# Eight weighted key rows summed by one strided reduction instead of three adds

## The reference

```
kx     = modulated_linear(x, s, k_aff_w, k_aff_b, k_w, k_b).reshape(B, N, 16, 8)
scores = einsum('bnhd,bnjd->bnhj', kx, kx) / sqrt(8)
A      = softmax(scores, axis=-1)
out    = einsum('bnhj,bnjd->bnhd', A, kx).reshape(B, N, 128)
```

## Time and profile before

| | |
|---|---|
| time, median of 3 runs | 597.94 us (597.91 to 598.32) |
| profiled execution | 596.94 us, span 595.1 us |
| busy: TensorE matmul | 575.1 us (97%), 4516 instructions |
| busy: VectorE | 483.7 us (81%), 1026 |
| busy: ScalarE | 372.0 us (63%), 855 |
| busy: GpSimd | 288.1 us (48%), 248 |
| VectorE's three adds of eight rows, L349, L358, L360 | 52.4, 19.2 and 13.9 us, 32 of each |
| GpSimd's three adds, L1063 | 116.8 us, 96 |
| mean granted clock of TensorE | 0.989 |

### The profile page before, as it was taken

The page is one execution under the profiler, slowest core; times in us unless marked ns, Lnnn a source line. Parts: engine busy times, 40 slices in busy tenths (PEclk is TensorE's granted clock), DMA queues, the critical chain, the costliest instruction groups (busy, mean ns, idle before and its releaser), DMA issues. The chain is left out here.

```text
span 595.1 us, 15251 instructions
## 1 busy us (share of the span) xinstructions
PE 575.1 (97%) x4516; PEld 492.3 (83%) x4516; DVE 483.7 (81%) x1026; ACT 372.0 (63%) x855; POOL 288.1 (48%) x248
## 2 busy tenths in 40 slices
PE   8999999999999999999999999999998997799998
PEld 8888888888888888888888888888887896466775
DVE  4235888898989898988889898989898788777776
ACT  1767767777777677777777767777775321534443
POOL 1011666666666666666666666666666563000000
PEclk9999999999999999999999999999999977999999
DMA  7300000000000000000000000000000000000004
GB/s 240 86 2 2 1 3 2 0 0 0 0 0 0 0 0 0 0 0 0 0 0 0 0 0 0 0 0 0 0 0 2 1 1 0 1 1 0 0 0 141
DMA packets 9364, 7.18 MB, mean 12 GB/s; under 512 B 1089, under 2 KB 8833, under 8 KB 9217
## 3 DMA queue, kind: packets, MB, share of 16 engines
q1 hardware_dynamic: 9344, 6.94, 3.9%
HBM read 4.84 MB, written 2.10 MB: 12 GB/s over the span
## 5 line engine op out<-in xcount | busy, mean ns | idle before, releaser
L1068 POOL TENSOR_TENSOR pair<-kx 128x1152 f32<-128x1152 f32 x32 | 82.2, 2568 | 167.4 <-DVE shifted L388 158.4
L580 PE MATMUL bank_a<-v,prob 128*128 128x65 f32 x1024 | 128.5, 274 | 1.5 <-ACT prob L814 0.8
L580 PEld LDWEIGHTS bank_a<-v,prob 128*128 128x128 f32 x1024 | 121.8, 192 | 6.3 <-ACT prob L814 3.2
L1063 POOL TENSOR_TENSOR mix_hi<-mix_hi 128x512 f32<-128x512 f32 (+2 forms) x96 | 116.8, 1217 | 7.5
L271 DVE TENSOR_REDUCE row_max<-bank_s 128x4 bf16<-128x512 f32 x128 | 88.9, 694 | 26.2 <-PE bank_s L555 25.3
L814 ACT ACTIVATE prob<-bank_t 128x512 f32<-128x512 f32 x128 | 68.9, 589 | 6.9 <-PE bank_t L570 4.7
L587 PE MATMUL misc<-yT,wq_sb 128*128 128x128 f32 x512 | 69.6, 279 | 0.5 <-DVE yT L419 0.5
L570 PE MATMUL bank_t<-qT,kT 64*128 64x256 f32 x512 | 65.7, 376 | 0.0
L1056 POOL TENSOR_TENSOR mix_hi<-weight,kx 128x1024 f32<-128x1024 f32 x32 | 64.1, 2002 | 3.1 <-ACT weight L814 3.1
L282 DVE TENSOR_TENSOR att<-bank_a,recip_den 128x256 f32<-128x256 f32 x128 | 54.4, 425 | 13.0
L587 PEld LDWEIGHTS misc<-yT,wq_sb 128*128 128x128 f32 x512 | 62.0, 191 | 3.6 <-DVE yT L419 0.7
(11 more groups left out here) (149 smaller groups left out, 998.9 us busy)
## 6 DMA issues: line engine op xcount, KB each, us to landing
out<-acc_all SPq DMA_DIRECT2D x8, 256.0 KB, 2.3
x_all<-in_xT SPq DMA_DIRECT2D x1, 1024.0 KB, 9.7
w_sb<-in_w SPq DMA_DIRECT2D x2, 512.0 KB
x_all<-in_xT SPq DMA_DIRECT2D x1, 768.0 KB, 7.5
wq_sb<-in_wq SPq DMA_DIRECT2D x1, 512.0 KB, 6.1
wpost_sb<-in_wpost SPq DMA_DIRECT2D x1, 512.0 KB, 9.6
x_all<-in_xT SPq DMA_DIRECT2D x1, 256.0 KB, 3.3
b_rows<-in_b SPq DMA_DIRECT2D x16, 4.0 KB
```

Source lines behind the costliest of these rows:

```text
L580: last = mm(att_bank(g)[:, w, :], prob[:, g % 2, w, :], v1[:, j, g, :], start=(w == 0), stop=True, skip_group_check=True)
L1063: G.tensor_tensor(mix_hi[:, 0:r, :], mix_hi[:, 0:r, :], mix_hi[:, r:2 * r, :], ALU.add).then_inc(s_hi, 1)
L1068: G.tensor_tensor(pair[:, :, :], bass.AP(kx2, jc * 2 * P, [[4 * P, P], [0, SHIFTS], [1, P]]), bass.AP(kx2, jc * 2 * P, [[4 * P, P], [MD, S ...
```

## The change

VectorE's three adds over `mix_lo` become one `tensor_reduce`. It reads all eight rows, with the rows as the innermost axis (128 outputs of 8 elements, each 128 elements apart in memory), and writes the sum to a new tile `mix_part` of 128 x 128. It stands where the first of the three adds stood, ahead of L353. The other two adds, which stood behind the reciprocal, go. `mixed()` reads `mix_part` in place of the first row of `mix_lo`. The semaphore `s_lo` now counts two steps a sequence, not four, and VectorE's and ScalarE's waits on it are changed to match. GpSimd's half is as it was.

```
+        mix_part = sb("mix_part", [P, P])
...
                 if D:
-                    dve.wait_ge(s_lo, 4 * d + 1)
-                    V.tensor_tensor(mix_lo[:, 0:4, :], mix_lo[:, 0:4, :], mix_lo[:, 4:8, :], ALU.add).then_inc(s_lo, 1)
+                    dve.wait_ge(s_lo, 2 * d + 1)
+                    V.tensor_reduce(mix_part[:, :], mix_lo[:, :, :].rearrange("p r f -> p f r"), AX.X,
+                                    ALU.add).then_inc(s_lo, 1)
...
                     V.reciprocal(h_rden[:, :], h_den[:, :]).then_inc(s_hrden, 1)
-                    dve.wait_ge(s_lo, 4 * d + 2)
-                    V.tensor_tensor(mix_lo[:, 0:2, :], mix_lo[:, 0:2, :], mix_lo[:, 2:4, :], ALU.add).then_inc(s_lo, 1)
-                    dve.wait_ge(s_lo, 4 * d + 3)
-                    V.tensor_tensor(mix_lo[:, 0, :], mix_lo[:, 0, :], mix_lo[:, 1, :], ALU.add).then_inc(s_lo, 1)
                 def mixed():
                     if D:
-                        dve.wait_ge(s_lo, 4 * d + 4)
+                        dve.wait_ge(s_lo, 2 * n(d))
                         dve.wait_ge(s_hi, 4 * d + 4)
-                        V.tensor_tensor(mix_sum[:, :], mix_lo[:, 0, :], mix_hi[:, 0, :], ALU.add).then_inc(s_msum, 1)
+                        V.tensor_tensor(mix_sum[:, :], mix_part[:, :], mix_hi[:, 0, :], ALU.add).then_inc(s_msum, 1)
...
-                    need(act, s_lo, 4 * n(c - 2))
+                    need(act, s_lo, 2 * n(c - 2))
```

## The result

The changed kernel takes 604.21 us (median of 4 runs, 602.43 to 604.34) against 597.96 us for the kernel before: a ratio of 1.0096, 95% interval 1.0077 to 1.0116. It is slower by 6.2 us; the forecast was 600.2 us with a range of 594.8 to 603.5. The profiled execution took 602.43 us with a span of 600.6.

What follows compares the result with a forecast made beforehand. TensorE, busy 99.58 us of each 100 in the batch loop, was taken to bound it; +4.7 us in the loop and -2.4 at its end made +2.3 on the 597.94 us median: 600.2 us, range 594.8 to 603.5.

Steps and rivals of the forecast that it cites:

- The path: In a loop round, VectorE's addition to x, queued behind the exchanged instruction, feeds ScalarE's x1s, exponentials, then TensorE's weight load.
- the prediction's own signs of being wrong: Reduction under 1.75 us (no hole) or over 2.1, or a hole on TensorE without the round growing.
- The reduction: VectorE's new strided reduction of 1024 columns: 155 ns plus 1.73 ns per column as in L383, 1.93 us.
- the prediction's bounds: Length of VectorE's new reduction by the three strided reductions profiled: 1.86 to 1.97 us.
- the stride costs nothing: Rival: the reduction runs as if dense, 1.21 us, no loop hole, end gains 3.1: 594.8 us; chance 0.11.
- dearer step: Rival: the longer step makes the reduction 2.64 us, loop loses 23 us, end gains 1.7: 619 us; chance 0.11.
- held: Rival: GpSimd holds the reduction like the add, 2.89 us, loop loses 30 us, end gains under 1: 627; chance 0.06.
- The slack of TensorE's load: In a loop round, TensorE's load of the first exponential could go 0.10 us sooner, absorbing that much delay.
- The loop: Addition to x 0.28 us later, less 0.10 slack, leaves a 0.18 us TensorE hole in 26 rounds: +4.7 us.
- The cover: In a round the sum of both halves comes some 0.7 us sooner, costed at nothing because TensorE takes mix later.
- The hole is absorbed: Rival: time lost at TensorE's load only shortens its other waits, the loop keeps its time: 595.5 us; chance 0.18.
- The end of the batch loop: Reduction to score reduction takes 2.02 us, not 4.41, so what follows comes 2.4 us sooner (up to 3.4).

Runs made afterwards that it cites:

- The delay without a reduction: Kernel before, three adds kept, plus a small dense reduction nobody reads that delays the addition to x by 0.3 us: 604.61 us.
- the exchanged order: Changed kernel with the addition to x ahead of the strided reduction in VectorE's queue: 595.24 us.
- the delays: Kernel before with an unread extra reduction ahead of the addition to x, delaying it by 0.3 us (604.61 us) or by 0.07 us (598.64 us).
- measured alone: Kernel before with the strided reduction only in the last two slots, the three adds everywhere else: 595.06 us.

## Why the prediction was right and wrong

**The path** was right: reduction, addition to x, x1s, first exponential, TensorE's load. The delay without a reduction and the exchanged order show it from both sides: with the addition to x later by 0.3 us a round grows by 0.26 us though no reduction stands there, and with it ahead of the reduction a round is 0.01 us longer than before. The links between are read in the timelines. None of the prediction's own signs of being wrong came up; the size failed all the same.

**The reduction** was costed at 1.93 us and takes 1.965 in the loop: (1965 - 155) / 1024 = 1.77 ns per column, at the upper of the prediction's bounds (L434) and not at L383. That is 0.035 us a round, 0.9 us in all. GpSimd hardly holds it: 1.97 us beside GpSimd's adds, 1.90 with GpSimd idle (503.49), where the add it replaces took 1.65 and 0.69. The rivals "the stride costs nothing", "dearer step" and "held" fall.

**The slack of TensorE's load** is the step that failed: "So the load could go at 307.99, and it goes at 308.09: 0.10 us of slack." The 0.64 us from the start of the exponentials to the load were read in a late round, 462.75 to 463.39. There the load itself carries the wait for the exponential. In the 26 rounds it does not: the wait stands in a queue instruction of its own ahead of it, and the load goes 0.70 us after the exponentials begin (311.82 to 312.52). The profile calls this idle time "issue", not a wait for the exponential, and in the kernel before it did not show, since the load came 0.71 to 0.75 us after them in these rounds. So the slack was 0.03 to 0.04 us, by the delays, and 0.06 to 0.07 us a round, 1.7 us in all, were missed. The same holds one step earlier: the product of x1s was taken to be in time, and in the changed kernel its load goes 0.11 us after x1s ends, with idle time before it, but the load of the exponential is later still and sets the round.

**The loop** was forecast at +4.7 us. The trace has +7.5: the addition to x ends 0.313 us later, and less the slack that is 26 x (0.313 - 0.034) = 7.3. The two terms above give about the same, 4.7 + 0.9 + 1.7 = 7.3.

**The cover** held: mix_sum comes 0.5 us sooner in a round (0.7 was forecast), and TensorE takes no advantage. **"The hole is absorbed"** falls: the rounds grow by as much as the load is late.

**The end of the batch loop** was forecast at -2.4 (to -3.4) and measured alone at -2.9. In the changed kernel's own trace the score reduction comes 2.4 us sooner too, but then the last fillers took 5.39 us where they had taken 4.50, which gave back 0.9 before the last mix was taken, and the stretch of the experts gave back 0.6. The prediction had no term for either: it took the last round as covered. How much of the end's gain the timed runs of the changed kernel kept can't be read: the profiled execution is 1.8 us shorter than the other three runs.

**Sum**: in the profiled executions +7.5 in the loop and -2.0 everywhere else make the span 5.5 us longer (600.6 against 595.1); the medians of the timed runs differ by 6.2. Forecast were +4.7 and -2.4. The sign was right, the size was 2.7 times too small. Of the miss of 4.0 us the loop has 2.8, and the largest single part, 1.7, is the latency of one wait, read at a load that was not the load in question; the reduction has 0.9. The other 1.2 lie outside the 26 rounds; the changed kernel's trace has the fillers and the experts there, and the timed runs cannot tell.

Two kernels here beat both: the changed one with the addition to x ahead of the reduction (595.24 us) and the kernel before with the reduction in the last two slots only (595.06 us). They are faster than the kernel before by 0.25% to 0.60% and by 0.25% to 0.66%.

## What to carry to other kernels

An instruction that is replaced by a cheaper sum can still be dearer than its first part: look at what stands behind it in the queue and who waits for that, not at the total. A slack of a tenth of a microsecond has to be read at the very instruction in question: the same line in a slot that is written out, or for the next head group of the same round, answered its signal 0.05 to 0.07 us sooner here. Where a trace has not yet made an instruction wait, its latency is not on show, and a range has to allow for that. Where a long instruction has no one waiting for it, put the short one that others wait for in front of it, but only if its inputs are there: here VectorE waited 1.0 to 1.1 us for them, which the kernel with the reduction could afford and the kernel with the three adds could not quite.

## What the runs showed of the hardware that was not expected

A step of 128 words costs a VectorE reduction about the same as the steps of 8, 16 and 32 words: 1.70 to 1.77 ns per column against 1.67 to 1.77, and 1.03 densely. A product that writes with a step of 8 words pays about as much: 2.37 us against 1.52 for 1024 columns. A tensor_reduce of 1024 columns hardly feels GpSimd (1.97 us beside it, 1.90 alone). A TensorE load that carries the wait for an exponential itself started 0.05 us after the exponential's end; with that wait in a queue instruction of its own ahead of the load it was 0.11 to 0.12 us, in the hardware loop and outside it. On VectorE the same difference was 0.03 against 0.10 us, between the product and the sum that waits for it.
